# Output projection of an attention layer as three single-pass products, with its weights and the query weights split on other engines

## What is computed

```
x = x + cross_attention(layernorm(x), ctx)      # 25088 context rows, gate at its end
x = x + attention(layernorm(x))                 # 16 heads of 64, half-causal mask
x = x + ffn(layernorm(x))                       # shared SwiGLU + 32 experts, top 1

def attention(x):
    q, k, v = x @ Wq + bq, x @ Wk + bk, x @ Wv + bv       # Wq, Wk, Wv: 512 x 1024
    attn = softmax(mask(q k^T / 8))                       # per head
    return concat(attn v) @ Wo                            # Wo: 1024 x 512
```

## Time and profile before

| | us |
|---|---|
| median of 3 executions | 1160.43 |
| lowest, highest | 1158.77, 1161.05 |
| the profiled execution | 1158.48 |
| its span in the trace | 1156.7 |
| TensorE busy in the span | 1029.5 (89%) |
| VectorE busy | 627.4 (54%) |
| ScalarE busy | 381.9 (33%) |
| GpSimd busy | 17.4 (2%) |

### The profile page before, as it was taken

The page is one execution under the profiler, slowest core; times in us unless marked ns, Lnnn a source line. Parts: engine busy times, 40 slices in busy tenths (PEclk is TensorE's granted clock), DMA queues, the critical chain, the costliest instruction groups (busy, mean ns, idle before and its releaser), DMA issues.

```text
span 1156.7 us, 17000 instructions
## 1 busy us (share of the span) xinstructions
PE 1029.5 (89%) x6800; PEld 716.0 (62%) x6800; DVE 627.4 (54%) x981; ACT 381.9 (33%) x553; POOL 17.4 (2%) x23
## 2 busy tenths in 40 slices
PE   8999999999999999999999999999876765666666
PEld 8867888888888888888866856554432222222223
DVE  4457888888878878878757356221121111111112
ACT  2434466456456456456445352000000000000000
POOL 1000000000000000000013000000000000000000
PEclk9999999999999999999999999999999899889889
DMA  9447787787787787787794667999999999999997
GB/s 356 182 146 267 273 314 276 279 305 285 273 311 279 275 310 281 280 304 279 278 409 163 255 255 283 426 426 427 427 425 426 428 428 428 427 427 427 428 429 293
DMA packets 90690, 381.49 MB, mean 330 GB/s; under 512 B 5536, under 2 KB 6176, under 8 KB 74016
## 3 DMA queue, kind: packets, MB, share of 16 engines
q1 hardware_dynamic: 90656, 381.00, 84.5%
HBM read 355.29 MB, written 25.69 MB: 329 GB/s over the span
## 4 chain that ended last, share of the span: by engine, by line
DMA 47%; PE 26%; DVE 18%; SPq 3%; ACT 2%; issue 2%; DVEq 0%; ACTq 0%
DMA wide<-in_r_up 17%; DMA strips<-turned 11%; DMA pt<-strips 10%; DMA deep<-in_r_down 9%; DVE nat_lo L1309 4%; DVE pt_lo L1314 4%; DVE turned L1336 4%; SPq L359 3%; PE ps L999 3%; DVE st L1321 2%; PE ps L1013 2%; ACT pt_hi L1081 2%; PE ps L558 2%; PE ps L993 1%; PE ps L1027 1%
## 5 line engine op out<-in xcount | busy, mean ns | idle before, releaser
L572 PE MATMUL ps<-ctt_hi,q_hi 128*128 128x512 f32 x392 | 153.7, 392 | 0.0
L574 PE MATMUL ps<-ctt_hi,q_lo 128*128 128x512 f32 x392 | 152.6, 389 | 0.0
L573 PE MATMUL ps<-ctt_lo,q_hi 128*128 128x512 f32 x392 | 152.5, 389 | 0.0
L585 PE MATMUL ps<-nat_hi,pt_hi 128*128 128x512 f32 x368 | 143.5, 390 | 0.8 <-DVE pt_lo L1314 0.8
L586 PE MATMUL ps<-nat_lo,pt_hi 128*128 128x512 f32 x368 | 143.2, 389 | 0.0
L587 PE MATMUL ps<-nat_hi,pt_lo 128*128 128x512 f32 x368 | 143.2, 389 | 0.0
L1253 ACT ACTIVATE sg<-ps 128x256 f32<-128x256 f32 x32 | 12.3, 383 | 389.4 <-PE ps L993 389.4
L1661 DVE TENSOR_TENSOR hh<-sg,ps 128x256 f32<-128x256 f32 x32 | 13.5, 421 | 231.4 <-PE ps L999 231.4
L1013 PE MATMUL ps<-deep,hh_t 128*32 128x512 f32 x496 | 76.3, 742 | 53.7 <-DMA deep<-in_r_down 52.2
L1304 DVE TENSOR_TENSOR ctt_lo<-ctt,ctt_hi 128x2048 fp32r<-128x2048 f32 x49 | 110.3, 2288 | 15.7 <-ACT ctt_hi L1073 15.7
L1077 ACT ACTIVATE nat_hi<-nat 128x2048 fp32r<-128x2048 f32 x48 | 92.1, 1918 | 77.7 <-DMA nat<-in_ctx_rows 77.7
(11 more groups left out here) (301 smaller groups left out, 1324.7 us busy)
## 6 DMA issues: line engine op xcount, KB each, us to landing
wide<-in_r_gate SPq DMA_DIRECT2D x32, 2048.0 KB, 25.9
wide<-in_r_up SPq DMA_DIRECT2D x32, 2048.0 KB, 27.4
deep<-in_r_down SPq DMA_DIRECT2D x31, 2048.0 KB, 25.7
ctt<-in_ctx_t SPq DMA_DIRECT2D x49, 1024.0 KB, 7.5
nat<-in_ctx_rows SPq DMA_DIRECT2D x48, 1024.0 KB, 7.2
strips<-turned SPq DMA_DIRECT2D x96, 256.0 KB, 5.2
pt<-strips SPq DMA_DIRECT2D x24, 1024.0 KB, 4.8
w_gate<-in_w_g_t SPq DMA_DIRECT2D x2, 1024.0 KB, 14.4
```

What stands on the lines that cost most here:

```text
L572: mm(o, qh, ctt_hi[par][:, c, :], start=(c == 0), stop=False)
L573: mm(o, qh, ctt_lo[par][:, c, :], start=False, stop=False)
L574: last = mm(o, ql, ctt_hi[par][:, c, :], start=False, stop=(c == HC - 1))
L585: mm(o, p_hi[:, w, :], n_hi[:, t, :], start=(first and t == 0), stop=False)
```

## The change

- The output projection is made of three products too. ScalarE rounds w_o in two instructions (`output_hi`, the first ahead of its copies of the queries, the second behind them), VectorE subtracts in two (`output_lo`, the first behind the key weights, the second behind two of the key columns).
- ScalarE's copy of a pair's products now rounds (`o_hi`), and VectorE subtracts it from PSUM bank 4 (`out_lo`), for pair c-2 between the two `head_norm` of pair c, and for pairs 6 and 7 behind the loop. The next products wait for both, and so does each output part.
- The low part of the query weights is computed by VectorE, ahead of that of the key weights, and no longer by GpSimd.
- w_o is loaded where tile 0 was (after `end_products`). Tile 0 goes out after the queries, tile 1 after the keys, tiles 2 to 4 after the values, tile 5 after the last pair's products, tiles 6 and 7 after the output projection.
- The semaphores of w_vs and w_gate1 are joined to one, and those of the low parts are regrouped.

The two lists of semaphore names are left out of the diff.

```diff
@@ -31,6 +31,7 @@
 SB = 3
+OL = 4
 E = 32
@@ -125,7 +126,8 @@
         q_t = at("q_t", [P, AC, NQ], F32, small)
-        o_t = at("o_t", [P, AC, NQ], F32, small)
+        o_hi = at("o_hi", [P, AC, NQ], F32R, small)
+        o_lo = at("o_lo", [P, OL, NQ], F32R, small + 41152 + 3 * D * 4)
         k_t = at("k_t", [P, AC, NQ], F32, small + 24768)
@@ -217,13 +219,15 @@
         w_q_hi = at("w_q_hi", [P, HC, DA // 2], F32R, RINGB + 4 * WB)
-        w_o = at("w_o", [P, AC, D], F32, RINGB + 2 * 3 * WB)
+        w_o = at("w_o", [P, AC, D], F32, RINGB + 5 * WB)
+        w_o_lo = at("w_o_lo", [P, AC, D], F32R, RINGB + 5 * WB)
+        w_o_hi = [at(f"w_o_hi{h}", [P, AC // 2, D], F32R, RINGB + 4 * WB + (1 - h) * (WB // 2)) for h in range(2)]
...
-        tile_at = [RINGB + 5 * WB, RINGB + 4 * WB, RINGB + 7 * WB, low_at, RINGB + 8 * WB, RINGB + 3 * WB, low_at + WB, RINGB + 6 * WB]
+        tile_at = [RINGB + 6 * WB, RINGB + 7 * WB, low_at, RINGB + 8 * WB, RINGB + 3 * WB, low_at + WB, RINGB + 5 * WB, RINGB + 4 * WB]
         wide = [at(f"wide{p}", [P, HC, FI], F32, tile_at[p]) for p in range(NR)]
@@ -396,8 +400,8 @@
             sp.wait_ge(s["scores_ready"], NB)
-            sp.dma_start(w_vs[:, :, :], chunks(a["w_vs_t"])).then_inc(s["wvs_loaded"], 16)
-            sp.dma_start(w_gate1[:, :, :], chunks(a["w_g_t"][0:D, :])).then_inc(s["wg1_loaded"], 16)
+            sp.dma_start(w_vs[:, :, :], chunks(a["w_vs_t"])).then_inc(s["wvsg_loaded"], 16)
+            sp.dma_start(w_gate1[:, :, :], chunks(a["w_g_t"][0:D, :])).then_inc(s["wvsg_loaded"], 16)
             sp.dma_start(flat(w_v), runs(a["w_v"])).then_inc(s["wv_loaded"], 16)
@@ -417,23 +421,24 @@
             sp.wait_ge(s["end_products"], 2 * QT)
-            load_turn(0, 0)
+            sp.dma_start(w_o[:, :, :], chunks(a["w_o"])).then_inc(s["wo_loaded"], 16)
             sp.wait_ge(s["c2s_in_psum"], QT)
...
             sp.wait_ge(s["qa_in_psum"], AC)
-            sp.dma_start(w_o[:, :, :], chunks(a["w_o"])).then_inc(s["wo_loaded"], 16)
-            load_turn(0, 1)
+            load_turn(0, 0)
             sp.wait_ge(s["ka_in_psum"], AC)
             sp.dma_start(wd_shared[:, :, :], chunks(a["s_down"])).then_inc(s["dsh_loaded"], 16)
+            load_turn(0, 1)
+            sp.wait_ge(s["va_in_psum"], 4)
             load_turn(0, 2)
-            sp.wait_ge(s["va_in_psum"], 4)
-            for k in range(3):
-                load_turn(1, k)
+            load_turn(1, 0)
+            load_turn(1, 1)
             sp.wait_ge(s["aot_in_psum"], AC)
+            load_turn(1, 2)
+            sp.wait_ge(s["ao_in_psum"], 2)
             load_turn(2, 0)
-            sp.wait_ge(s["ao_in_psum"], 2)
             load_turn(2, 1)
@@ -509,10 +514,7 @@
                 pool.tensor_tensor(w_v_lo[:, part, :], w_v[:, part, :], w_v_hi[:, part, :].bitcast(F32),
-                                   ALU.subtract).then_inc(s["wvqlo_ready"], 1)
-            pool.wait_ge(s["whi_ready"], 5)
-            pool.tensor_tensor(w_q_lo[:, :, DA // 2:], w_q[:, :, DA // 2:], w_q_hi[:, :, :].bitcast(F32),
-                               ALU.subtract).then_inc(s["wvqlo_ready"], 1)
+                                   ALU.subtract).then_inc(s["wvlo_ready"], 1)
@@ -722,7 +724,7 @@
                 pe.wait_ge(s["acct_ready"], t + 1)
-                pe.wait_ge(s["wvs_loaded"], 16)
+                pe.wait_ge(s["wvsg_loaded"], 32)
                 for c in range(HC):
@@ -735,7 +737,7 @@
                 pe.wait_ge(s["c2st_ready"], t + 1)
-                pe.wait_ge(s["wg1_loaded"], 16)
+                pe.wait_ge(s["wvsg_loaded"], 32)
                 for c in range(HC):
@@ -787,7 +789,7 @@
-            pe.wait_ge(s["wvqlo_ready"], 2)
+            pe.wait_ge(s["wvlo_ready"], 2)
             for n in range(2):
@@ -797,7 +799,7 @@
             project_tile(1, by_chunk(2, AC), w_q, a_t, range(AC // 2), s["qa_in_psum"])
-            pe.wait_ge(s["wvqlo_ready"], 3)
+            pe.wait_ge(s["wlo_ready"], 1)
             pe.wait_ge(s["at_ready"], 3)
@@ -808,7 +810,7 @@
                 last.then_inc(s["qa_in_psum"], 1)
-            pe.wait_ge(s["wklo_ready"], 2)
+            pe.wait_ge(s["wlo_ready"], 3)
             for o in range(4):
@@ -839,7 +841,8 @@
                 if c:
-                    pe.wait_ge(s["aot_ready"], c)
+                    pe.wait_ge(s["ohi_ready"], c)
+                    pe.wait_ge(s["olo_ready"], c)
                 heads = [(ps[DK * k:DK * (k + 1), 4, :], 2 * c + k) for k in range(2)]
@@ -850,8 +853,15 @@
-                pe.wait_ge(s["aot_ready"], c + 1)
-                last = mm(ps[:, 3 + 2 * t, :], o_t[:, c, t * P:(t + 1) * P], w_o[:, c, :], start=(c == 0), stop=(c == AC - 1))
+                h = c // (AC // 2)
+                pe.wait_ge(s["ohi_ready"], c + 1)
+                pe.wait_ge(s["olo_ready"], c + 1)
+                pe.wait_ge(s["wlo_ready"], 4 + h)
+                o, oh, ol = ps[:, 3 + 2 * t, :], o_hi[:, c, t * P:(t + 1) * P], o_lo[:, c % OL, t * P:(t + 1) * P]
+                wh, wl = w_o_hi[h][:, c % (AC // 2), :], w_o_lo[:, c, :]
+                mm(o, oh, wh, start=(c == 0), stop=False)
+                mm(o, oh, wl, start=False, stop=False)
+                last = mm(o, ol, wh, start=False, stop=(c == AC - 1))
                 if c == AC - 1:
@@ -873,7 +883,6 @@
             pe.wait_ge(s["va_ready"], 4)
-            pe.wait_ge(s["wo_loaded"], 16)
             for c in range(2, AC):
@@ -1205,10 +1214,17 @@
             a_columns(1)
+
+            def output_hi(h):
+                act.activation(w_o_hi[h][:, :, :], w_o[:, h * AC // 2:(h + 1) * AC // 2, :], ACT.Copy).then_inc(s["whi_ready"], 1)
+
+            act.wait_ge(s["wo_loaded"], 16)
+            output_hi(0)
             for o in range(AC):
...
                                bias=b_q[:, o:o + 1]).then_inc(s["qa_ready"], 1)
+            output_hi(1)
@@ -1224,7 +1240,7 @@
                 act.wait_ge(s["aot_in_psum"], c + 1)
-                act.activation(o_t[:, c, :], ps[:, 4, 0:NQ], ACT.Copy).then_inc(s["aot_ready"], 1)
+                act.activation(o_hi[:, c, :], ps[:, 4, 0:NQ], ACT.Copy).then_inc(s["ohi_ready"], 1)
@@ -1520,11 +1536,14 @@
             a_rest(1)
+            dve.wait_ge(s["whi_ready"], 5)
+            dve.tensor_tensor(w_q_lo[:, :, DA // 2:], w_q[:, :, DA // 2:], w_q_hi[:, :, :].bitcast(F32),
+                              ALU.subtract).then_inc(s["wlo_ready"], 1)
             for h in range(2):
...
                 dve.tensor_tensor(w_k_lo[:, part, :], w_k[:, part, :], w_k_hi[:, part, :].bitcast(F32), ALU.subtract
-                                  ).then_inc(s["wklo_ready"], 1)
+                                  ).then_inc(s["wlo_ready"], 1)
@@ -1546,13 +1565,30 @@
-            for o in range(6):
+            def out_lo(c):
+                dve.wait_ge(s["ohi_ready"], c + 1)
+                dve.tensor_tensor(o_lo[:, c % OL, :], ps[:, 4, 0:NQ], o_hi[:, c, :].bitcast(F32), ALU.subtract
+                                  ).then_inc(s["olo_ready"], 1)
+
+            def output_lo(h):
+                part = slice(h * AC // 2, (h + 1) * AC // 2)
+                dve.wait_ge(s["whi_ready"], 6 + h)
+                dve.tensor_tensor(w_o_lo[:, part, :], w_o[:, part, :], w_o_hi[h][:, :, :].bitcast(F32), ALU.subtract
+                                  ).then_inc(s["wlo_ready"], 1)
+
+            output_lo(0)
+            for o in range(2):
+                key_columns(o)
+            output_lo(1)
+            for o in range(2, 6):
                 key_columns(o)
...
             for c in range(AC):
-                for h in range(2 * c, 2 * c + 2):
-                    head_norm(h)
+                head_norm(2 * c)
+                if c >= 2:
+                    out_lo(c - 2)
+                head_norm(2 * c + 1)
                 if c == 0:
@@ -1560,6 +1596,8 @@
                     value_rows(2 + c)
+            out_lo(AC - 2)
+            out_lo(AC - 1)
             for t in range(QT):
```

More of the change, by code:

```diff
@@ L242, in perceiver_layer @@
         x_loaded0 x_loaded1 cols_loaded rows_loaded wqc_loaded wks_loaded wkc_loaded wqs_loaded wvc_loaded sel_loaded
-        wg2_loaded wg1_loaded wvs_loaded nat_loaded0 nat_loaded1 ctt_loaded0 ctt_loaded1 end_nat_loaded strips_stored pt_loaded wv_loaded wq_loaded wk_loaded wo_loaded
+        wg2_loaded wvsg_loaded nat_loaded0 nat_loaded1 ctt_loaded0 ctt_loaded1 end_nat_loaded strips_stored pt_loaded wv_loaded wq_loaded wk_loaded wo_loaded
         gsh_loaded ush_loaded dsh_loaded
@@ L255, in perceiver_layer @@
         acct_in_psum acct_ready c2s_in_psum c2s_ready c2st_in_psum c2st_ready gate_in_psum z_ready
-        gate_ready an_ready at_in_psum at_ready alo_ready whi_ready wvqlo_ready wklo_ready qa_in_psum qa_ready ka_in_psum ka_ready
+        gate_ready an_ready at_in_psum at_ready alo_ready whi_ready wvlo_ready wlo_ready qa_in_psum qa_ready ka_in_psum ka_ready
         va_in_psum va_ready
```

(2 more changed lines are left out.)

## The result

| | before | changed |
|---|---|---|
| median of 20 executions, us | 1160.97 | 1156.24 |
| lowest, highest | 1158.77, 1163.63 | 1154.38, 1159.24 |
| span of the profiled execution | 1156.7 | 1154.4 |

The ratio is 0.9964, with 0.9956 to 0.9972 as its 95% interval: 4.2 us less, between 3.3 and 5.1. The forecast was 1157.5, faster, with a range of 1155.4 to 1160.2.

What follows compares the result with a forecast made beforehand. The prediction took the end to follow from tile 8's issue, set by the engine chain reaching expert 0. Gains of 2.46 and 0.41 us, 2.87 off the profiled 1158.48, gave a median of 1157.5 us, range 1155.4 to 1160.2.

Steps and rivals of the forecast that it cites:

- What bounds the kernel: Whole kernel: the end follows a fixed time after the DMA engines never stop, from tile 8's issue at 711.96 us.
- Part 1: Cross-attention gate: query weights' low part leaves GpSimd, VectorE's multiply no longer stalls, TensorE's idle goes; 2.46 us gained (2.0 to 2.62).
- Part 2: Splitting w_o: two roundings on ScalarE and two subtractions on VectorE fall into idle time; cost nothing.
- Part 3: Output projection products: three float32r passes per part; TensorE's own time for a pair goes from 4.45 to 4.23 us.
- Part 4: Heads: the subtraction lengthens the ScalarE-VectorE round, 4.27 us expected (4.18 to 4.78); heads gain 0.41 us together.
- Rival 1: Heads: the round over ScalarE and VectorE becomes 4.78 us, eating the 2.46 gained; 1160.4 us; chance 0.12.
- rival 4: Heads: VectorE's late work delays the exponentials, each pair waits a further ScalarE turn, 5.2 us; 1162.5 us; chance 0.05.
- Part 5: Loads: three tiles behind the heads are through at 708.8 us, before tile 8's issue at 709.1; cost nothing.
- 2: Cross-attention gate: the 2.46 us don't arrive because another wait takes their place; only 0.4 remains, 1160.0 us; chance 0.12.
- 3: Output projection: the saved passes count almost in full; 6.0 us gained, 1154.4 us; chance 0.08.
- The sum: Whole kernel: 2.46 + 0.41 = 2.87 us off the profiled 1158.48; median 1157.5 us, 0.25% less.

Runs made afterwards that it cites:

- e6: Changed kernel with a fourth tile (tile 4) loaded behind the heads; 1160.98 us, ratio 1.0002 against the kernel before.
- e5: Changed kernel with VectorE's subtraction for a pair done twice; 1160.74 us, ratio 0.9995 against the kernel before.
- b0: The kernel before, unchanged, compared with itself; 1161.67 us, ratio 1.0001.
- e4: Changed kernel, each output part waiting for its pair's low part only ahead of its third product; 1156.08 us, ratio 0.9962 against the kernel before.
- e2: Changed kernel with the query weights' low part moved back to GpSimd; 1160.85 us, ratio 0.9990 against the kernel before.
- e1: Kernel before with only the query weights' low part moved from GpSimd to VectorE; 1158.13 us, ratio 0.9962 against the kernel before.
- k1: Kernel before with TensorE's idle time ahead of the transposes of `an` filled by 40 small matmuls; 1159.78 us, ratio 0.9988 against the kernel before.
- a1: The changed kernel measured a third time, nothing altered; 1158.79 us, ratio 0.9966 against the kernel before.
- e7: Changed kernel with the late low-part wait, and the wait for the last value rows moved later too; 1156.24 us, ratio 0.9948 against the kernel before.
- b1: The kernel before measured once more, unchanged, against itself; 1162.07 us, ratio 1.0004.

## Why the prediction was right

**What bounds the kernel: right.** B to the end is 444.2 to 445.0 us in eleven of the thirteen other traces, whatever was changed ahead of B. The exceptions are e6, which moves a tile on purpose, and e5, 1.0 us longer for a reason that I haven't followed up.

**Part 1, 2.46 us: right.** The traces give 2.57 when it is done alone and 2.56 when it is undone. The multiply, 3.31 us with GpSimd's subtraction beside it and 0.69 without, agrees with the rule of the Trainium skill cited there (SBUF — State Buffer, Who interferes with whom). Not all of it is explained: the multiply ends 0.54 us after GpSimd, and the addition at the other place 0.55 us (608.77 to 609.32), less than the 0.69 us that either takes alone. What the step may have lacked is a second gain: behind such idle time the granted clock fell to half in one of five profiles, which b0's rows show. The forecast had no term for it. Whether it is part of why the median came out 1.3 us below the forecast isn't shown.

**Part 2, nothing: right.** No engine waits for w_o or for one of the low parts of the weights. The second subtraction of w_o delays two key columns by 0.12 us (they follow the first two after 3.00 us, 643.97 to 646.97, where it was 2.88, 645.62 to 648.50), less than the 0.3 foreseen, and nobody waits for them.

**Part 3, TensorE's own round 4.23 us: mis-sized.** The two parts of a pair save 0.15 and 0.09 us, 0.24 together, where 0.22 had been taken (0.18 and 0.04). But e4 shows a round of 4.13: without the early wait the output part also starts 0.25 us behind the start of the first transposes, where that was 0.34 before and 0.37 in the changed kernel. This 0.09 the prediction didn't have; 4.45 - 0.24 - 0.09 = 4.12. The page of the Trainium skill that was weighed there (FP8 and Floating Point Precision, TensorE Precision Notes) counts four passes for true FP32. The step from it to time, that three passes save a quarter or 3.4 us, was the prediction's own, and it doesn't hold here: a part falls from 0.86 to 0.77 us, or from 1.05 to 0.90, by 10 to 14%. The count of four itself is not contradicted: 0.86 / 4 is 0.215 us, near the 0.23 us between the starts of following float32r products. All that isn't part 1 gave 0.52 (e2), and with the late wait 0.51 + 1.37 = 1.88, near the 1.8 by the rows, though waits are still in it.

**Part 4, the link: right.** Rounds of 4.24 us against 4.27, the last pair 4.24 against 4.22. At the end the subtraction of pair 7 stands openly before the last parts, as the prediction put it, and e4 wins half a microsecond there. The heads give 0.51 us against 0.41, and the agreement holds piece by piece, if all of part 1's 2.57 is taken off ahead of them: 0.13 up to the first second transposes (0.04 foreseen), 0.86 in four rounds (0.72), -0.32 in the last (-0.30), 0.16 in the run of three parts (0.21), and -0.33 at the end (-0.26). e5 shows that the link sets the round, and e4 that TensorE's own work is only 0.11 us shorter. Rival 1 (4.78 us), and rival 4 (5.2) on top of it, were wrong in price: they add the copy to a round of 3.92 that held it already, as the rows of the last pair show.

**Part 5, nothing: right, with 1.45 us to spare.** Tile 8 was expected at 709.1 by the clock of the old trace. It came at 709.85 in a trace that began this stage 0.97 us later, thus at 708.9. The 1.45 us are worked out from e6, not read from a row. The 1.2 us from issue to flow had no good source: it is the distance to a window's edge, and in the trace of before 213 GB/s already flow from 696 to 697 us, so it is shorter.

**Rivals.** 1 and 4 fall by the rounds of 4.24 us, 2 by e1, 3 by the parts' measured costs.

**The sum.** 2.57 + 0.51 = 3.08 us from A to B and 0.19 behind it make 3.3. The median gave 4.2 (3.3 to 5.1), the two repetitions 5.3 and 4.0. The direction, the split of the gain over the parts and the place of each were as forecast. The median's surplus of about 1 us isn't explained: the clock behind the idle time is a candidate that k1 supports weakly.

## What to carry to other kernels

- Compare one instruction with itself: 3.31 us in one place and 0.69 in another, with the same shape, told more than any share of busy time. Then look which engine was at work meanwhile. GpSimd was busy for 2% of the span, and one of its instructions was worth more than the whole new projection.
- When a product is split into hi and lo, put the wait for lo ahead of the product that reads it, not ahead of the group. The wait at the group's head put an extra instruction into a loop over three engines, left it open at the end, and cost 1.37 us.
- Where spans vary by 5 us from one execution to the next ahead of the change, read traces between two fixed events. Here that stretch repeats to 0.1 us for the same kernel, but for the one profile in which the clock fell, and resolves steps that 20 executions can't.

## What the runs showed of the hardware

- VectorE's multiply with two SBUF inputs ended 0.54 us after GpSimd's subtraction, in before and in e2 alike. Beside GpSimd's instruction of 4.53 us it took 2.62 us longer than alone. The blocking goes both ways: VectorE's addition of two SBUF inputs took 2.15 us beside GpSimd's first subtraction for the values, and GpSimd's second took 5.00 where the first took 4.54 (the changed kernel; before: 2.14, 5.00 and 4.53).
- A 128x512 float32 product took 0.86 to 0.87 us, a float32r product 0.23 us behind another one, and three of them as a group of their own 0.77 to 0.90.
- After 2.49 us of idle time TensorE's granted clock fell once in five profiles to half (1.2 GHz), one to two microseconds after work had begun again, and stayed there for about three. The other four idle times, of 2.46 and 2.47 us, passed without it.
- In the profiles of e1, a1, e7 and b1 the granted clock was 0.91 in the first 20 us, and these four reach A at 604.8 to 606.6 us; the ten others, at 1.00 there, reach it at 601.3 to 604.1.
